# Expert stage in 31 tiles of 256 and nine of 128 rows, with the result rows worked out inside the stage

## The reference, cut to what matters

```python
h_flat = h.reshape(-1, D)                                  # 4096 tokens x 256
probs = softmax(h_flat @ router_w)                         # 8 experts
gates, idx = top_k(probs, 2); gates = gates / gates.sum(-1, keepdims=True)
hid  = relu(einsum('nd,edf->nef', h_flat, exp_w1) + exp_b1)   # 256 -> 1024
eout = einsum('nef,efd->ned', hid, exp_w2) + exp_b2           # 1024 -> 256
y = einsum('ned,ne->nd', eout, combine)                    # combine holds the gates
return x + y.reshape(x.shape)
```

## Time and profile before

| | us |
|---|---|
| three runs: median (lowest to highest) | 1425.97 (1422.19 to 1427.66) |
| the profiled execution, its own time | 1427.18 |
| its span in the profile | 1425.4 |
| first tile's transposes begin, in the span | 144.33 |
| last matmul of the expert stage begins | 621.26 |
| one tile of the expert stage | 11.94 |
| busy in the whole span: PE, PEld, DVE, ACT, POOL | 1276.8, 1160.8, 988.0, 903.1, 665.1 |

### The profile page before, as it was taken

One profiled execution on the slowest core, in us unless ns is written; L12 is line 12 of the kernel. 1 busy time (PEld: TensorE's weight loads), 2 busy tenths in 40 slices (PEclk: granted clock), 3 DMA queues, 4 the chain that ended last, 5 costly groups with the idle time before them and its releaser, 6 DMA issues. The chain is left out here.

```text
span 1425.4 us, 34480 instructions
## 1 busy us (share of the span) xinstructions
PE 1276.8 (90%) x9923; PEld 1160.8 (81%) x9923; DVE 988.0 (69%) x2764; ACT 903.1 (63%) x2319; POOL 665.1 (47%) x580
## 2 busy tenths in 40 slices
PE   5884899999999999945899999999999999999996
PEld 4774899999999999944587888778877878788885
DVE  5776688889878987743776667566766667666652
ACT  3442677778777877722566676666666666667671
POOL 2775577787778777743032332332232232231221
PEclk9999999999999999976899999999999999999997
DMA  5885121121112111128766656655675556654620
GB/s 189 271 274 187 46 66 46 57 61 51 57 48 65 54 56 58 49 89 253 225 214 184 190 182 198 205 181 162 195 220 182 177 179 204 199 189 148 202 72 15
DMA packets 184707, 203.18 MB, mean 143 GB/s; under 512 B 18176, under 2 KB 172736, under 8 KB 184576
## 3 DMA queue, kind: packets, MB, share of 16 engines
q1 hardware_dynamic: 169136, 161.57, 36.9%
q10 hardware_dynamic: 9264, 23.47, 5.1%
q0 software_dynamic: 6176, 16.79, 3.4%
HBM read 155.89 MB, written 41.68 MB: 139 GB/s over the span
## 5 line engine op out<-in xcount | busy, mean ns | idle before, releaser
L1254 ACT ACTIVATE bias<-bias,neg_max 128x256 f32<-128x256 f32 x512 | 255.4, 501 | 193.7 <-DVE neg_max L1586 191.6
L343 POOL TENSOR_TENSOR w_lo<-w,w_hi 128x512 fp32r<-128x512 f32 x156 | 242.2, 1572 | 0.0
L1586 DVE CUSTOM_DVE_ANT_0 bias<-ps_s,bias 128x256 f32<-128x256 f32 x512 | 194.5, 417 | 34.0 <-PE ps_s L1351 21.4
L745 DVE TENSOR_TENSOR w_lo<-w,w_hi 128x512 fp32r<-128x512 f32 x156 | 149.8, 999 | 68.7 <-ACT w_hi L423 67.0
L544 PE MATMUL ps_y<-w_hi,hidT_hi 128*128 128x256 f32 x624 | 180.2, 289 | 1.9 <-DVE token_rows L759 1.9
L531 PE MATMUL ps_h<-htokT_hi,w_hi 128*128 128x256 f32 x624 | 178.5, 286 | 3.2 <-DVE htokT_lo L750 3.2
L531 PE MATMUL ps_h<-htokT_lo,w_hi 128*128 128x256 f32 x624 | 178.2, 286 | 0.0
L531 PE MATMUL ps_h<-htokT_hi,w_lo 128*128 128x256 f32 x624 | 178.1, 285 | 0.0
L1349 PE MATMUL ps_s<-mask_f,minus_ident 128*128 128x256 f32 x512 | 154.3, 323 | 25.6 <-DVE neg_max L1586 15.8
L544 PE MATMUL ps_y<-w_lo,hidT_hi 128*128 128x256 f32 x624 | 177.0, 284 | 0.0
L544 PE MATMUL ps_y<-w_hi,hidT_lo 128*128 128x256 f32 x624 | 177.0, 284 | 0.0
(11 more groups left out here) (276 smaller groups left out, 3496.9 us busy)
## 6 DMA issues: line engine op xcount, KB each, us to landing
bias<-bias_dram SPq DMA_DIRECT2D x128, 512.0 KB, 4.2
w<-w_dram ACTq DMA_DIRECT2D x32, 512.0 KB
xin<-dispatch SPq DMA_DIRECT2D x39, 256.0 KB, 2.8
expert_out<-token_rows SPq DMA_DIRECT2D x39, 256.0 KB, 2.2
q_stack<-q_hi_rows SPq DMA_DIRECT2D x64, 128.0 KB, 2.9
q_stack<-q_lo_rows SPq DMA_DIRECT2D x64, 128.0 KB, 2.9
k_stack<-k_hi_rows SPq DMA_DIRECT2D x60, 128.0 KB, 2.8
k_stack<-k_lo_rows SPq DMA_DIRECT2D x60, 128.0 KB, 2.8
```

The lines of the kernel that those rows point to most:

```text
L343: pool.tensor_tensor(w2_part["lo"][:, k, :], w2_piece(e, k), w2_part["hi"][:, k, :].bitcast(F32), ALU.subtract).then_inc(sem("w2_split"), 1)
L745: dve.tensor_tensor(w1_part["lo"][:, k, :], w1_piece(e, k), w1_part["hi"][:, k, :].bitcast(F32), ALU.subtract).then_inc(sem("w1_split"), 1)
L1254: act.activation(head_rows(h, j), head_rows(h, j), ACT.Exp, scale=-1.0, bias=neg_max[par][:, h, j:j + 1], accum_out=total[par][:, h, j:j + ...
L1586: dve.tensor_tensor_reduce(head_rows(h, j), ps_s[h % 2][:, j * T:(j + 1) * T], head_rows(h, j), -1.0, LARGEST, ALU.add, ALU.min, neg_max[p ...
```

## The change

The tiles become two kinds: `PAIRS` = 31 of 256 rows, then `SINGLES` = 9 of 128. `tokens(t)` gives a tile's rows; every instruction on tokens, hidden parts and results is cut to them. The weights are split for all 40 tiles as before, in pieces of full size. The 256-row tiles are given out first, as whole pairs of 128-row units of each expert up to 31, and the rest goes to the small ones. The table therefore needs more steps. In small tiles VectorE does the rounded copies of the hidden pairs 1 and 3 instead of ScalarE. `out_row` leaves its place before the stage: VectorE computes it in four parts of 16 choices after `take_out` in bodies 26 to 29, in 14 dependent steps each, with the block of zeros as scratch memory; for that it waits for `pad_sent` before its first body. The hardware loop has six rounds (before: eight), and bodies 26 to 40 are written out. The second layer's gather is told the new length.

```diff
-TILES = (K * B * T - TOK) // TOK + E
+PAIRS = (K * B * T // P + E - 1 - (E + 1)) // 2
+SINGLES = E + 1
+TILES = PAIRS + SINGLES
+OUT_ROWS = PAIRS * TOK + SINGLES * P
...
+def tokens(t):
+    return TOK if not isinstance(t, int) or t < PAIRS else P
...
     def load(tile):
-            sp.dma_start(htok[tile.par], dispatch[bass.ds(row, TOK), :]...)
+            m = tokens(tile.t)
+            sp.dma_start(htok[tile.par][:, 0:m // P, :], dispatch[bass.ds(row, m), :]...)
...
     # ScalarE
             if a_tile(t):
                 upper_w2(t, e, 0)
-                round_hidden(t, 1)
+                if tokens(t) == TOK:
+                    round_hidden(t, 1)
                 upper_w2(t, e, 1)
                 upper_w2(t, e, 2)
-                round_hidden(t, 3)
+                if tokens(t) == TOK:
+                    round_hidden(t, 3)
                 upper_w2(t, e, 3)
...
     # TensorE: up, and in down likewise  for j in range(tokens(t) // P)
-                        last = pe.matmul(ps_h[f // 2][:, (f % 2) * TOK:(f % 2 + 1) * TOK],
-                                         w1_part[a][...], htokT[b][:, c, :],
+                        last = pe.matmul(ps_h[f // 2][:, (f % 2) * TOK:(f % 2) * TOK + tokens(t)],
+                                         w1_part[a][...], htokT[b][:, c, 0:tokens(t)],
...
     # VectorE, before the stage
-        dve.wait_ge(sem("h2T_ready"), B)
-        every = chosen_all[:].rearrange("p b q -> p (b q)")
-        s.then(dve.tensor_tensor(big, spread(every, [P, B * K * J, E], 2), spread(slot8, [P, B * K * J, E], 1), ALU.is_equal))
-        s.then(dve.tensor_tensor(big, big, spread(delta[:], [P, B * K * J, E], 1), ALU.mult))
-        s.then(dve.tensor_reduce(every, big, X, ALU.add))
-        s.then(dve.tensor_tensor(every, every, row_all[:].rearrange("p b q -> p (b q)"), ALU.add))
-        s.did(dve.tensor_copy(out_row[:], chosen_all[:]))
+        def place_rows(part):
+            n = B * K * J // PLACE_STEPS                    # 16; shape = [P, 16, 8]
+            def pick(out, kind):
+                s.then(dve.tensor_tensor(picked_one, which, spread(delta[:, kind, :], shape, 1), ALU.mult))
+                s.then(dve.tensor_reduce(out, picked_one, X, ALU.add))
+
+            s.then(dve.tensor_tensor(which, spread(chosen, shape, 2), spread(slot8, shape, 1), ALU.is_equal))
+            pick(parted[:], 2)
+            pick(moved[:], 1)
+            s.then(dve.tensor_tensor(parted[:], rows, parted[:], ALU.is_ge))
+            s.then(dve.tensor_scalar(moved[:], moved[:], float(PAIRS * TOK), None, ALU.add))
+            pick(chosen, 0)
+            s.then(dve.tensor_tensor(moved[:], moved[:], chosen, ALU.subtract))
+            s.then(dve.tensor_tensor(moved[:], moved[:], parted[:], ALU.mult))
+            s.then(dve.tensor_tensor(chosen, chosen, rows, ALU.add))
+            s.then(dve.tensor_tensor(chosen, chosen, moved[:], ALU.add))
+            s.did(dve.tensor_copy(out_row[:].rearrange("p b q -> p (b q)")[:, at], chosen))
...
     # VectorE, body
             if a_tile(t):
                 split_hidden(t, 0)
+                if tokens(t) < TOK:
+                    round_hidden(t, 1)
                 split_hidden(t, 2)
+                if tokens(t) < TOK:
+                    round_hidden(t, 3)
             if a_tile(t - 1):
                 take_out(tile.ahead(-1))
+            if isinstance(t, int) and PAIRS - 1 - PLACE_STEPS <= t < PAIRS - 1:
+                place_rows(t - (PAIRS - 1 - PLACE_STEPS))
+
+        dve.wait_ge(sem("pad_sent"), 16 * E)
         tile_loop(dve, body)
...
-    rounds = (TILES - 3) // UNROLL - 1
+    rounds = (PAIRS - 4) // UNROLL
```

More of the change, by code:

```diff
@@ L181, in condition_and_route @@
     row_i = sb("row_i", [P, B, K * J], U32)
-    tiles_n = sb("tiles_n", [P, E])
-    tiles_cum = [sb(f"tiles_cum{i}", [P, E]) for i in range(2)]
-    delta = sb("delta", [P, E])
+    units = [sb(f"units{i}", [P, 2, E]) for i in range(2)]
+    own = sb("own", [P, 2, E])
+    used = sb("used", [P, 2, E])
+    singles = sb("singles", [P, E])
+    delta = sb("delta", [P, 3, E])
     pad_row = sb("pad_row", [1, E], I32)
@@ L201, in condition_and_route @@
     b2 = [b2_rows[:, i, :] for i in range(2)]
-    big = columns[:, 0, :].rearrange("p (q e) -> p q e", e=E)
     tiles = columns[0:1, 1, 0:TILES * E].rearrange("p (t e) -> p t e", e=E)
@@ L517, in turn_in @@
             for c in range(C):
-                for j in range(J):
+                for j in range(tokens(t) // P):
                     last = pe.transpose(ps_t[:, c * TOK + j * P:c * TOK + (j + 1) * P], htok[tile.par][:, j, c * P:(c + 1) * P], ident)
@@ new lines, in _ @@
+        every, halves = own[:, 0, :], own[:, 1, :]
+        s.then(dve.tensor_tensor(every, count[:], first_row, ALU.subtract))
+        s.then(dve.tensor_scalar(every, every, float(P - 1), 1.0 / P, ALU.add, ALU.mult))
+        s.then(dve.tensor_scalar(every, every, -(P - 1) / (2.0 * P), MAGIC, ALU.add, ALU.add))
+        s.then(dve.tensor_scalar(every, every, -MAGIC, None, ALU.add))
+        s.then(dve.tensor_scalar(halves, every, 0.5, -0.25, ALU.mult, ALU.add))
+        s.then(dve.tensor_scalar(halves, halves, MAGIC, -MAGIC, ALU.add, ALU.add))
@@ L704, in _ @@
             now = 1 - now
[L705 to L712 removed]
+        cum_units, cum_pairs = units[now][:, 0, :], units[now][:, 1, :]
@@ new lines, in _ @@
+        ends, begins = used[:, 0, :], used[:, 1, :]
+        left = units[1 - now][:, 0, :]
+        s.did(dve.tensor_scalar(ends, cum_pairs, float(PAIRS), None, ALU.min))
+        s.then(dve.tensor_tensor(begins, cum_pairs, halves, ALU.subtract))
+        s.did(dve.scalar_tensor_tensor(delta[:, 0, :], begins, float(TOK), first_row, ALU.mult, ALU.subtract))
+        s.then(dve.scalar_tensor_tensor(singles[:], ends, -2.0, cum_units, ALU.mult, ALU.add))
+        s.then(dve.tensor_scalar(begins, begins, float(PAIRS), None, ALU.min))
@@ new lines, in _ @@
+        s.then(dve.tensor_tensor(ends, ends, begins, ALU.subtract))
+        s.then(dve.scalar_tensor_tensor(left, ends, -2.0, every, ALU.mult, ALU.add))
+        s.then(dve.tensor_tensor(left, singles[:], left, ALU.subtract))
+        s.did(dve.scalar_tensor_tensor(delta[:, 2, :], ends, float(TOK), first_row, ALU.mult, ALU.add))
+        s.then(dve.tensor_scalar(delta[:, 1, :], left, float(P), None, ALU.mult))
+        s.then(dve.tensor_tensor(delta[:, 1, :], delta[:, 1, :], delta[:, 2, :], ALU.subtract))
@@ new lines, in _ @@
+        kinds = ((slice(0, PAIRS), const[0:1, TILE_NO:TILE_NO + PAIRS], cum_pairs[0:1, :], delta[0:1, 0, :], float(TOK)),
+                 (slice(PAIRS, TILES), const[0:1, TILE_NO:TILE_NO + SINGLES], singles[0:1, :], delta[0:1, 1, :], float(P)))
+        dve.wait_ge(sem("back_done"), B)
+        for at, no, cum, _, _ in kinds:
+            shape = [1, no.shape[-1], E]
+            s.did(dve.tensor_tensor(tiles[:, at, :], spread(no, shape, 2), spread(cum, shape, 1), ALU.is_ge))
+        for at, no, cum, _, _ in kinds:
+            s.did(dve.tensor_scalar(tile_ok[:, at], no, cum[:, E - 1:E], None, ALU.is_lt))
@@ L715, in _ @@
         s.then(dve.tensor_tensor(tiles, spread(tile_e[:], [1, TILES, E], 2), spread(slot8[0:1, :], [1, TILES, E], 1), ALU.is_equal))
-        s.then(dve.tensor_tensor(tiles, tiles, spread(delta[0:1, :], [1, TILES, E], 1), ALU.mult))
-        s.did(dve.tensor_reduce(tile_row[:], tiles, X, ALU.add))
-        s.then(dve.tensor_scalar(tile_ok[:], tile_no, cum[0:1, E - 1:E], None, ALU.is_lt))
-        s.then(dve.scalar_tensor_tensor(tile_row[:], tile_no, float(TOK), tile_row[:], ALU.mult, ALU.subtract))
+        for at, no, _, less, _ in kinds:
+            last = dve.tensor_tensor(tiles[:, at, :], tiles[:, at, :], spread(less, [1, no.shape[-1], E], 1), ALU.mult)
@@ L721, in _ @@
+        s.did(last)
+        s.did(dve.tensor_copy(tile_tab[:, 0, :], tile_e[:]))
+        dve.wait_ge(sem("table_step"), s.at)
+        s.then(dve.tensor_reduce(tile_row[:], tiles, X, ALU.add))
+        for at, no, _, _, size in kinds:
+            last = dve.scalar_tensor_tensor(tile_row[:, at], no, size, tile_row[:, at], ALU.mult, ALU.subtract)
+        s.then(last)
         s.then(dve.tensor_tensor(tile_row[:], tile_row[:], tile_ok[:], ALU.mult))
-        s.did(dve.tensor_copy(tile_tab[:, 0, :], tile_e[:]))
@@ L731, in _ @@
-        s.did(dve.tensor_copy(out_row[:], chosen_all[:]))
+        def place_rows(part):
+            n = B * K * J // PLACE_STEPS
+            at = slice(part * n, (part + 1) * n)
+            rows = row_all[:].rearrange("p b q -> p (b q)")[:, at]
+            chosen = chosen_all[:].rearrange("p b q -> p (b q)")[:, at]
+            shape = [P, n, E]
+            which, picked_one = zeros[:].rearrange("p (i q e) -> p i q e", i=2, e=E)[:, 0, :, :], zeros[:].rearrange("p (i q e) -> p i q e", i=2, e=E)[:, 1, :, :]
+            def pick(out, kind):
[12 more added lines that the diff above has]
+            s.did(dve.tensor_copy(out_row[:].rearrange("p b q -> p (b q)")[:, at], chosen))
```

(1 more changed line is left out.)

63 lines of the change are left out of this document (35 added, 28 removed).

## The result

| | before | after |
|---|---|---|
| median of four runs, us (lowest to highest) | 1425.89 (1422.19 to 1427.66) | 1445.76 (1443.8 to 1448.32) |
| ratio, 95% interval | | 1.0144 (1.0115 to 1.0172) |
| the profiled execution, us (its span) | 1427.18 (1425.4) | 1443.96 (1442.2) |
| last matmul of the expert stage begins | 621.26 | 627.16 |
| from the first to the last store of the output | 657.2 | 667.8 |

The change makes the kernel 1.4% slower, where I forecast a gain of 3.6 us, and the time lies above my range. The last two rows of the table split the loss of the profiled execution: 5.9 us appear in the expert stage and 10.6 in the attention stage behind it, whose work the change leaves alone but for the addresses of the gathered rows.

The account below looks back on a forecast made before the run. TensorE was taken to bound the kernel's expert stage, with GpSimd's and VectorE's turns a hidden second bound. Small tiles +5.0, drain +4.6, result rows −6 gave 3.6 us saved, 1422.4 us; range 1410 to 1435.

Parts of the forecast that it names:

- Small tiles, +5.0: Expert stage: small tiles 9.6 us apart instead of 11.94 for large ones, 5.0 us saved up to the last tile's start.
- the turns: GpSimd and VectorE alternate by whole instructions; their holds, 9.2 us per small tile, exceed TensorE's 8.5 and become the bound.
- Drain, +4.6: From the last tile's start to the expert stage's end: 16.5 us instead of 21.1, 4.6 us saved.
- Table, wait for the zero rows, first load, 0: Before the first tile: longer table hidden by the first load, wait for zero rows costing nothing, at most 1 us.
- The result rows, −6 with 10 as the bound: Tiles 26 to 29: VectorE's 14 dependent steps each, 3.8 us a tile, cost 6 us in all, about 10 if steps wait.
- the dearer case: Tiles 26 to 29: each short step waits out a GpSimd turn; VectorE's tile 16 us, 4 over, about 10 in all.
- the first overrun: In the rows' dearer estimate, VectorE's first tile running 4 us over is absorbed; three more give about 10 us.
- the middle value of 6: Cost taken for the result rows, between nothing to 4 us with GpSimd idle and about 10 if steps wait turns.
- The same instructions gather the rows later: nothing: Later gathering of the result rows by unchanged instructions was said to cost nothing.
- The rivals: Three alternatives: TensorE stays the bound (1412 us, 0.24), rows at full price (1426, 0.11), engines in series (1436, 0.18).
- The full price of the rows: Rival: nearly every short result-row step waits behind a GpSimd turn, 10 us, all else as forecast; 1426 us; chance 0.11.
- In series: Rival: GpSimd and VectorE work one after the other in small tiles, period 11.0 us; 1436 us; chance 0.18.

Follow-up runs that it names:

- experiment 8: Changed kernel, result rows ahead of first tile, one more loop round; in small tiles GpSimd computes only 32 of 512 columns of lower w2 pieces: 1401.94 us, ratio 0.9846.
- 7: Changed kernel, result rows ahead of first tile, one more loop round; in small tiles GpSimd does the first lower w2 piece before hidden pair 1: 1419.64 us, ratio 0.9953.
- 2: Changed kernel with 116 met waits on ScalarE between expert and attention stages, moving its attention loop: 1433.73 us, ratio 1.0064.
- 3: Kernel before, eight more tiles written out and 12 met waits on ScalarE, its attention loop placed as in the changed kernel: 1440.13 us, ratio 1.0109.
- 13: Changed kernel, rows ahead of first tile, two rounded copies back on ScalarE, ScalarE filled with 80 instructions, VectorE with 36 met waits: 1414.6 us, ratio 0.9929.
- 14: Changed kernel, rows ahead of first tile, 116 met waits on ScalarE, plus 92 met waits on VectorE behind the expert stage: 1428.07 us, ratio 1.0026.
- 4: Changed kernel with result rows ahead of the first tile and 116 met waits on ScalarE behind the expert stage: 1415.76 us, ratio 0.9928.
- 1: Changed kernel with result rows worked out once ahead of the first tile, nothing in tiles 26 to 29: 1431.58 us, ratio 1.0051.
- 9: Changed kernel, rows ahead of first tile, one more loop round; rounded copies of pairs 1 and 3 back on ScalarE: 1416.3 us, ratio 0.9928.

## Why the prediction was wrong

- **Small tiles, +5.0**: right in mechanism and size. The period of 9.6 us is that of the turns: with GpSimd's work gone it is 8.43 (experiment 8), with GpSimd's order changed it stays (7). Without the rows the 39 periods save 8 × 11.94 − 11.73 − 11.30 − 65.95 = 6.5 us; the first small-to-small period, 8.43, is the one that beats 9.6.
- **Drain, +4.6**: measured +5.0.
- **Table, wait for the zero rows, first load, 0**: right. The table ends 138.28 against 135.94, the load is issued at 141.58 against 141.55, and tile 24 begins 0.4 us earlier than before, not later.
- **The result rows, −6 with 10 as the bound**: the step that failed inside the stage; measured −17.8. I had VectorE's tile right in the dearer case (16 us; TensorE's periods of 16.05 and 16.60), but for a reason that holds in one part of four. In the first part four steps do wait out turns (2.7 us in all), and yet the period in which it lies is only 0.6 longer. In the other three the steps take no turns; there it is VectorE's long instructions behind them that meet GpSimd's. The periods are longer by 0.6, 4.1, 4.7, 1.7 and 6.7: the first overrun is absorbed, as I had it, and the next are the 4 of the dearer case. What lies above my bound of 10 is nearly all the half clock, 6.9 us, for which I charged nothing though the earlier trace rows had shown it behind a pause of 1.9. And the middle value of 6 rested on short steps that meet GpSimd idle and so cost little; three parts met it idle, but an idle GpSimd was the sign that all waited for VectorE. The lock that the Trainium skill describes ("SBUF — State Buffer", section "SBUF: two separate sides") would, I wrote, make most steps wait. The trace agrees with the rule, but not with my use of it: the two-input steps of the first part wait (up to 1.26 us instead of 0.29), in the other parts GpSimd held nothing at the time, and experiments 7 and 8 agree for the long instructions (1.50 us beside GpSimd, 0.69 alone).
- **"The same instructions gather the rows later: nothing"**: the other half of the loss, 10.6 us, is in no term and no rival. The gathers are indeed the same; it is the code that moved. Experiments 2, 3, 13 and 14 change nothing but places of code, and the time between the stores moves by 11.1, 13.7, 8.6 and 8.2 us (3 has eight tiles written out besides, which do the same work); 4 against 1 moves it by 16.3.
- **The sum**: with rows at −17.8, stage +11.5 and attention −10.6 it gives −16.9; the profiled executions differ by 16.8. The medians differ by 19.9; the 3 us between, within the spread of the runs, are not traced.
- **The rivals**: none was right. The full price of the rows came nearest in the mechanism, with 10 us against 17.8, but said 1426. "In series" gave 1436, a time nearer the measured than mine, but with small tiles of 11.0 us that did not come.

Repaired, the change does what it says: ratios of 0.9928 (4), 0.9928 (9) and 0.9929 (13), 10 us below the kernel before. My forecast without the rows' price was 9.6 us. That the two are so close is partly luck: the moved rows cost 1.8 us at the start, the small tiles save 1.5 more than forecast, and the attention stage of 4 is 2.3 us shorter than before for a reason that was not looked for.

Open: what rule gives the bad places. That the loop touches four pieces of 128 instructions instead of three fits ScalarE's number of fetches at the six places tried (20 at 2, 38, 54 and 98 past, 40 at 66 and 81), but only if the pieces begin 82 to 92 past the multiples of 128 as counted here (a loop of 283 touches four from 102 past the begin of a piece on). It does not fit the price at 81, and not VectorE, which stalls at 84 with no more fetches than elsewhere. Whether a fetch of another engine's code stands in the way was not tried.

## What to carry to other kernels

Idle time of an engine in a balanced loop is mostly the time in which it waits for the others; work added to it is paid whole, with the pauses' half clock on top. Put such work where the pipeline is empty anyway, here beside the first load. And when a change adds or removes written-out code ahead of a hardware loop, compare the idle time without a reason at the loop's jumps and the number of instruction packets before judging the change itself: here the place of the code was worth as much as the change. Filling put in to move a loop costs its own time where the engine has no idle time: nothing that shows on ScalarE here, about 5 us on VectorE.

## What the runs showed of the hardware

- A hardware loop of 283 recorded ScalarE instructions stalls 4.2 us at each jump back where its code begins 66 past a multiple of 128 instructions (three kernels), about 1 us at 81, and not at 2, 38, 54 or 98. By the store-to-store times a stall of 4.2 costs 2.8 to 4.1 us of the whole, half clock included.
- VectorE's loop of 369 recorded instructions stalls 2.1 to 2.5 us once a round, ahead of one copy, where it begins 84 past (two kernels), without additional fetches. Another 2.4 to 2.7 us ahead of its first operation are there in the good kernels as well.
- A step of 128x128 with two inputs in SBUF lasts 0.29 us on VectorE beside an idle GpSimd and up to 1.26 beside a subtraction of GpSimd; a reduction of one input lasts 0.29 beside either.
- A met wait as filling: VectorE passes 92 of them in 9.1 us, at the end of the expert stage, where it has no time to spare. On ScalarE 116 of them behind the expert stage cost nothing that shows: from the stage's last matmul to the first output store it is 144.5 us with them and 144.6 without.
- A matmul of 128 moving columns stands 0.11 us from the next behind a weight load of 128 columns, one of 256 columns 0.12: halving a tile's tokens saves next to nothing in the half where they are what moves and the weights change with every matmul.
